# An attention and mixture-of-experts block: the softmax denominators given out by heads, and the shared expert's order in the second part changed

## The chip, the cores and the metric

The kernel is one program on one core of a Trainium2 chip. The metric is the device time of one execution in microseconds. The engines are PE (matmuls), DVE, ACT and POOL (elementwise and scalar work) and SP, whose queue issues most DMAs; they run side by side and wait for each other through semaphores.

## What is computed

The input is x, 4 batches of 512 rows of 512, and a context of 1601 rows a batch: 257 image rows and 1344 text rows. The block adds cross attention and then a mixture of experts.

```
q = rms_norm(LN(x) Wq + bq);  k, v from text rows;  k_img, v_img from image rows
attn = softmax(q k'/sqrt(32)) v  +  softmax(q k_img'/sqrt(32)) v_img      (16 heads of 32)
x = x + attn Wo + bo
h = LN(x)
router: sigmoid(h Wr), 8 groups, the best 3 of them, the best 4 of 32 experts, weights normed
each expert takes its first 80 tokens:  out[token] += w * (silu(h Wg) * (h Wu)) Wd
x = x + out + shared expert: (silu(h Sg) * (h Su)) Sd
```

The image and the text softmax have a denominator each, for every head and query.

## The kernel before

**Attention.** One batch after another goes through a projection stage and an attention stage. In the attention stage keys stand on partitions in 13 tiles of 128 (n = 0 to 12, in ORDER): n=0 is an image tile, n=1 the last 65 image rows, n=2 is mixed (its first 64 rows are text, the others image), and n=3 to 12 are text. The 16 heads are taken in 4 groups of 4. A step s is one tile of one group, and there are 52 steps a batch. In each step
- `scores(s + 2)` issues 12 f16 matmuls on PE: three products for each of 4 heads. A head has a row strip of the array (32 rows, all 128 columns), and the results go to two of three pairs of banks;
- ACT makes the exponentials of a step in two instructions (line 566), into one of four buffers `prob`;
- `weighted(s)` waits for the exponentials of step s (`a_exp`) and issues the numerators (line 1046): for each head an f32 matmul of the tile's values (up to 128 rows, 32 columns) with 512 queries. A head has a column strip of the array (all rows, 32 columns) and 32 partitions of bank NUM;
- the denominators (line 1053) are matmuls of the same form into bank DEN, with ones as weights. For image tiles and the mixed tile they read `prob` in steps n=0, 1 and 2, four heads each. For text tiles DVE first adds up the exponentials of n=3 to 12 in `sums`; the product with ones comes in the next group, at n=6 for the first 256 queries and at n=8 for the others, four heads each. For a batch's last group it stands behind the last step.

In the mixed step n=2 the numerators of the image half (rows 64 to 127) are issued, then the denominators over all 128 rows. DVE copies the image numerators out of NUM (line 764, `a_ni`). In n=3 the numerators of the mixed tile's text half follow, ahead of the tile's own. ACT waits for `a_av` before it overwrites a buffer of four steps ago; for the mixed tile it waits for the count of the step behind it, because that step reads the buffer last. The instructions on PE are in program order, written out by hand.

**The second part** (`ffn_program`) begins at about 967 us. It finishes the attention's output for the last batch (`output`, `out_rows`), norms its four row blocks and turns them for use as matmul operands:

- `out_norm(j)` on DVE writes `xn[j % 2]`, `norm_high` on ACT and `norm_low` on DVE split it into two f16 halves in `xs[j % 2]`, `turn_out(j)` on PE turns them, and SP stores xn to `table` in DRAM. With two buffers, out_norm(2) waits for the store of block 0 (`s_tab`).
- SP's queue holds, in this order: the input rows, the router's weights, a turned block, the three residual loads `x1s` (1 MB each), three of four parts of the weight ring (1.5 MB each), a wait, the fourth, and then the four stores.
- `gate_up(n)` on PE, n = 0 to 15, is 24 matmuls for quarter n % 4 of block n // 4; ACT makes a tanh (`gate_tanh`), DVE multiplies (`gate`, two instructions), ACT makes the high half and DVE the low half of `hs` (`gate_high`, `gate_low`).
- `down(bk)` on PE waits for all four quarters of its block (`f_lo`) and makes four products of 12 matmuls; DVE adds each to the residual (`residual`), and SP stores the result.
- Between these, DVE works out the router's choice in a long row of small instructions. From it come the slots: `one_hot(j)` on DVE makes a table for 128 tokens in one of two buffers, and `slots_of(j)` on PE multiplies it in (5 matmuls). ACT copies the sums out (`arow`), a DMA turns them, DVE makes indices (`e_idx`), and POOL gathers the experts' rows.
- POOL writes `ioS` by iota (2560 elements a partition) once the attention's low halves are there (`t_lo`).

Behind it a loop over 32 experts gathers rows, multiplies them and adds them to the result by indirect DMAs.

## Time and profile before

| | us |
|---|---|
| median of 3 runs (lowest, highest) | 1386.26 (1382.42, 1392.75) |
| the profiled execution | 1390.19 |
| its span, first to last instruction | 1388.3 |
| mean granted TensorE clock | 0.964 |
| PE busy | 1237.4 (89%) |
| DVE busy | 889.4 (64%) |
| ACT busy | 667.9 (48%) |
| POOL busy | 184.3 (13%) |

Matmuls are pipelined, so that PE's busy time is not PE at its peak. Line numbers (L1046) are those of the kernel printed above. An f32 matmul stands in the trace as two records, so four of them are "x8". The durations of single records overlap; the time from one start to the next says more. A number in square brackets is the idle time before a row, with who ended it.

### The profile page before, as it was taken

What the parts mean: (1) busy time and instruction counts of PE and PEld (TensorE: products, weight loads), DVE (VectorE), ACT (ScalarE), POOL (GpSimd) and SP (SyncE); (2) the same over time, 40 slices, a digit from 0 to 9 for tenths busy, and PEclk for the clock granted to TensorE, in tenths of its full rate; (3) what the DMA queues carried; (4) which work ended last, traced back from release to release, by engine and by line L of the source; (5) the groups of instructions that cost most, each with busy time, mean ns of one, the idle gap of its engine ahead of it and who ended that gap; (6) DMA issues with size and microseconds to landing.
All of it is one profiled execution on the core that took longest, in us unless ns stands there. A gap on an engine that the chain in (4) does not pass through costs nothing. (4 is left out here: it accounts for less than half of the span.)

```text
span 1388.3 us, 22059 instructions
## 1 busy us (share of the span) xinstructions
PE 1237.4 (89%) x8916; PEld 460.8 (33%) x8916; DVE 889.4 (64%) x1169; ACT 667.9 (48%) x910; POOL 184.3 (13%) x299
## 2 busy tenths in 40 slices
PE   4988999999999899989989998995778998988986
PEld 2542222444222245422224442221433333333332
DVE  5765877777587878757688776886666653222221
ACT  4546886345788534578853448883211011111111
POOL 0210000132000013200001320000210001333332
PEclk9999999999999999999999999997979999999999
DMA  7200000221000112200011122010800102899884
GB/s 276 84 25 15 2 2 7 85 69 69 24 1 1 51 41 69 92 1 1 2 64 36 61 76 92 1 62 25 337 8 31 39 0 82 279 289 311 288 283 110
DMA packets 38388, 117.80 MB, mean 85 GB/s; under 512 B 6544, under 2 KB 6800, under 8 KB 33040
## 3 DMA queue, kind: packets, MB, share of 16 engines
q1 hardware_dynamic: 33168, 105.60, 21.5%
q0 software_dynamic: 5120, 10.82, 3.7%
q8 instruction: 68, 1.11, 0.3%
q14 instruction: 32, 0.26, 0.1%
HBM read 95.67 MB, written 20.73 MB: 84 GB/s over the span
## 5 line engine op out<-in xcount | busy, mean ns | idle before, releaser
L566 ACT ACTIVATE work<-ps 128x1024 f32<-128x1024 f32 (+1 forms) x416 | 403.1, 1021 | 61.0 <-PE ps L1039 58.7
L1046 PE MATMUL ps<-work,vals 128*32 128x512 f32 (+2 forms) x1792 | 236.6, 604 | 0.9 <-ACT work L566 0.8
L862 PE MATMUL ps<-wts,work 128*128 128x512 f16 x864 | 205.3, 389 | 14.6 <-DVE work L595 14.6
L1039 PE MATMUL ps<-quer,keys 32*128 32x512 f16 x2496 | 171.8, 377 | 25.1 <-ACT work L566 9.3
L778 DVE TENSOR_TENSOR work<-work 128x2048 f32<-128x2048 f32 x64 | 146.6, 2291 | 11.4 <-ACT work L566 7.3
L778 DVE TENSOR_TENSOR attn<-attn,work 128x2048 f32<-128x2048 f32 x64 | 146.6, 2290 | 10.8 <-ACT work L566 7.3
L862 PE MATMUL ps<-wts,hl 128*128 128x512 f16 x480 | 116.1, 395 | 23.2 <-DVE hl L595 23.2
L862 PEld LDWEIGHTS ps<-wts,work 128*128 128x128 f16 x864 | 83.7, 100 | 116.6 <-issue 16.9
L1039 PEld LDWEIGHTS ps<-quer,keys 32*128 32x128 f16 x2496 | 46.2, 92 | 214.5 <-ACT work L566 189.2
L1786 PE MATMUL f_ps<-wring,xgt 128*80 128x512 f32 x256 | 117.1, 601 | 0.0
L1372 ACT ACTIVATE yf<-f_ps,wc 80x512 f32<-80x512 f32 x32 | 21.9, 683 | 171.3 <-PE f_ps L1801 143.3
L418 POOL TENSOR_SCALAR small<-small 128x1 f32<-128x1 f32 x68 | 13.7, 201 | 651.1 <-ACT work L486 651.1
L486 ACT ACTIVATE work<-work 128x512 f32<-128x512 f32 x68 | 42.8, 630 | 116.4 <-DVE work L612 116.4
L481 ACT CAST work<-work 128x512 f16<-128x512 f32 x68 | 42.0, 617 | 105.8 <-DVE work L625 105.4
L625 DVE SCALAR_TENSOR_TENSOR work<-work,small,vec 128x512 f32<-128x512 f32 (+1 forms) x72 | 63.6, 883 | 43.7 <-POOL small L421 43.6
L631 DVE TENSOR_TENSOR work<-work 128x512 f16<-128x512 f32 x68 | 47.0, 692 | 44.5 <-ACT work L481 44.4
L862 PEld LDWEIGHTS ps<-wts,hl 128*128 128x128 f16 x480 | 47.0, 101 | 84.0 <-issue 38.3
L1046 PEld LDWEIGHTS ps<-work,vals 128*32 128x32 f32 (+2 forms) x1792 | 35.9, 107 | 105.6 <-issue 89.9
L1629 DVE SCALAR_TENSOR_TENSOR hh<-eg,f_ps 80x256 f32<-80x256 f32 x32 | 13.3, 417 | 85.4 <-ACT eg L1367 85.4
L1801 PE MATMUL f_ps<-wring,ht 128*80 128x512 f32 x128 | 63.0, 615 | 3.5 <-DVE ht L1633 0.8
L1294 POOL DMA_INDIRECT out<-yf,idx x32 | 45.6, 1426 | 145.0 <-DMA out<-yf,idx 93.1
L1786 PEld LDWEIGHTS f_ps<-wring,xgt 128*80 128x80 f32 x256 | 39.1, 153 | 73.5 <-issue 73.5
(208 smaller groups left out, 1445.7 us busy)
## 6 DMA issues: line engine op xcount, KB each, us to landing
wring<-in_wx SPq DMA_DIRECT2D x32, 1536.0 KB, 7.9
raw<-in_ctx SPq DMA_DIRECT2D x52, 256.0 KB, 2.8
work<-in_x SPq DMA_DIRECT2D x4, 1024.0 KB, 5.5
table<-nums SPq DMA_DIRECT2D x16, 256.0 KB, 2.3
out<-x1s SPq DMA_DIRECT2D x16, 256.0 KB, 2.3
work<-in_x SPq DMA_DIRECT2D x12, 256.0 KB, 4.9
x<-work SPq DMA_DIRECT2D x12, 256.0 KB, 2.0
x2t_rows<-nums SPq DMA_DIRECT2D x12, 256.0 KB, 2.5
```

The source lines that it names most:

```text
L481: act.copy(stack[i % 2][:, 0, :], kraw[i % 2]).then_inc(k_hi, 1)
L486: act.activation(junk, kraw[i % 2], ACT.Square, accum_out=ssq[i % 2]).then_inc(k_sq, 1)
L566: act.activation(prob[0:rows, s % PROBS, 2 * half:2 * half + 2, :], ps[0:rows, 2 * pair:2 * pair + 2, :], ACT.Exp, scale=SCALE).then_inc(a ...
L625: ins = dve.scalar_tensor_tensor(kraw[i % 2][a:z, :], kraw[i % 2][a:z, :], rin[i % 2][a:z, :], vec[a:z, weight, :], ALU.mult, ALU.mult)
L631: dve.tensor_tensor(stack[i % 2][:, 1, :], kraw[i % 2], stack[i % 2][:, 0, :], ALU.subtract).then_inc(k_lo, 1)
L778: dve.tensor_tensor(acc, acc, cur, ALU.add).then_inc(a_sum, 1)
L862: mm = pe.matmul(out, lhs(a, c)[:, cols], wts[:, w, z, c * D:(c + 1) * D], start=(k == 0), stop=(k == len(steps) - 1))
L1039: mm = pe.matmul(ps[:, 2 * pair + h % 2, :], k[h * HD:(h + 1) * HD, :], q[h * HD:(h + 1) * HD, :], start=(e == 0), stop=(e == len(terms) - 1))
L1046: mm = pe.matmul(ps[h * HD:(h + 1) * HD, NUM, :], vals[a:z, ORDER[n], g * P + h * HD:g * P + (h + 1) * HD], prob[a:z, s % PROBS, h, :], st ...
L1294: pool.indirect_dma_start(out=out[:, :], out_offset=bass.IndirectOffsetOnAxis(ap=idx[:, n - 1:n], axis=0), in_=yf[(n - 1) % 2][:, :], in_o ...
L1786: mm = pe.matmul(ps[0:CAP, 7 if u % 2 == 0 else 0, :], xgt[u % 2][:, c, :], wring[:, u, c * 512:(c + 1) * 512], start=(c == 0), stop=(c == ...
L1801: mm = pe.matmul(ps[0:CAP, 2 + u % 2, :], ht[u % 2][:, c, :], wring[:, u, 2048 + c * D:2048 + (c + 1) * D], start=(c == 0), stop=(c == 1))
```

## The change

In the attention stage:
- The image denominators of n=0 are issued for heads 0 to 2 in their own step and for head 3 at the start of n=1, behind the next scores and ahead of the wait for the exponentials. Those of n=1 are issued for heads 0 and 1 in their step and for 2 and 3 at the start of n=2. The signal `a_av` moves with them.
- In the mixed tile each numerator of one half of the rows is paired with the denominator of the other half: in n=2 the image numerators (rows 64 to 127) with the denominator over rows 0 to 63, for four heads in turn; the text numerators (rows 0 to 63) with the denominator over rows 64 to 127, heads 0 and 1 at the end of n=3, behind the tile's own numerators, and heads 2 and 3 at the start of n=4.
- The text denominators of the group before are issued for one head over all 512 queries in each of n=6, 7, 8 and 9.

In the second part:
- xn and xs have four buffers; out_norm and norm_high lose their waits, and one semaphore counts all four stores. The three residual loads move behind the stores in SP's queue, and every `residual` waits for all three.
- POOL's iota waits for the last turn (`n_turn`).
- gate_up(4) moves ahead of the down products of block 0, gate_up(8) ahead of those of block 1; DVE and ACT follow.
- A down product is split: `down_first` issues three of four chunks of the first two products ahead of the wait for the last low half, `down_last` the other two products.
- The slot search goes two row blocks at a time behind each gate_up, and slots 12 to 15 stand behind gate_up(13) and gate_up(14); DVE makes one_hot(12) to (15) behind gate(13) and gate(14) and their low halves, and the indices behind gate_low(15).
- PE no longer waits for all residuals before the experts.

```diff
...
-                def denominator(g, kind, src, rows, a=0, z=L, first=False, last=False):
-                    for h in range(4):
-                        mm = pe.matmul(ps[h * HD:(h + 1) * HD, DEN, a:z], ones[0:rows, kind, g, :],
-                                       src[0:rows, h, a:z], start=first, stop=last)
-                    return mm
+                def image_part(s, h, rows, first=False):
+                    return pe.matmul(ps[h * HD:(h + 1) * HD, DEN, :], ones[0:rows, 1, s // KT, :],
+                                     prob[0:rows, s % PROBS, h, :], start=first, stop=False)
+
+                def mixed_part(s, h, a, z):
+                    return pe.matmul(ps[h * HD:(h + 1) * HD, DEN, :], ones[a:z, 2, s // KT, :],
+                                     prob[a:z, s % PROBS, h, :], start=False, stop=False)
+
+                def text_part(g, h, last=False):
+                    return pe.matmul(ps[h * HD:(h + 1) * HD, DEN, :], ones[:, 0, g, :], sums[g % 2][:, h, :],
+                                     start=False, stop=last)
+
+                def mixed_text(s, h):
+                    numerator(s, h, 0, SPLIT, False, False)
+                    return mixed_part(s, h, SPLIT, P)
 
                 def weighted(s):
                     g, n = s // KT, s % KT
+                    if n == 1:
+                        image_part(s - 1, 3, P, first=(g == 0)).then_inc(a_av, 1)
+                    if n == 2:
+                        image_part(s - 1, 2, LAST)
+                        image_part(s - 1, 3, LAST).then_inc(a_av, 1)
+                    if n == 4:
+                        mixed_text(s - 2, 2).then_inc(a_av, 1)
+                        mixed_text(s - 2, 3).then_inc(a_av, 1)
                     pe.wait_ge(a_exp, unit(bb, 2 * s + 1))
                     if n == 0:
                         if g == 0:
@@ -1064,26 +1085,30 @@
                                 pe.wait_ge(n_out, xn(out_batch(bb - 1), QT - 1))
                         else:
                             pe.wait_ge(a_nt, gn(bb, g - 1))
-                        numerator(s, 0, P, True, False)
-                        denominator(g, 1, prob[:, s % PROBS, :, :], P, first=(g == 0)).then_inc(a_av, 1)
+                        numerators(s, P, True, False)
+                        for h in range(3):
+                            image_part(s, h, P, first=(g == 0))
                     elif n == 1:
-                        numerator(s, 0, LAST, False, False)
-                        denominator(g, 1, prob[:, s % PROBS, :, :], LAST).then_inc(a_av, 1)
+                        numerators(s, LAST, False, False)
+                        image_part(s, 0, LAST)
+                        image_part(s, 1, LAST)
                     elif n == 2:
-                        numerator(s, SPLIT, P, False, True).then_inc(a_img, 1)
-                        denominator(g, 2, prob[:, s % PROBS, :, :], P).then_inc(a_av, 1)
+                        for h in range(4):
+                            mm = numerator(s, h, SPLIT, P, False, True)
+                            mixed_part(s, h, 0, SPLIT)
+                        mm.then_inc(a_img, 1)
                     elif n == 3:
                         pe.wait_ge(a_ni, gn(bb, g))
-                        numerator(s - 1, 0, SPLIT, True, False)
-                        numerator(s, 0, P, False, False).then_inc(a_av, 1)
+                        numerators(s, P, True, False)
+                        mixed_text(s - 1, 0)
+                        mixed_text(s - 1, 1)
                     else:
-                        numerator(s, 0, P, False, n == KT - 1).then_inc(a_av, 1)
-                        if g > 0 and n in (6, 8):
+                        numerators(s, P, False, n == KT - 1).then_inc(a_av, 1)
+                        if g > 0 and 6 <= n < 10:
                             if n == 6:
                                 pe.wait_ge(a_sum, added(bb, g - 1, ADDS - 1))
-                            at = 0 if n == 6 else L // 2
-                            mm = denominator(g - 1, 0, sums[(g - 1) % 2], P, at, at + L // 2)
-                            if n == 8:
+                            mm = text_part(g - 1, n - 6)
+                            if n == 9:
                                 mm.then_inc(a_den, 1)
...
-        xn = [spare[:, j, :] for j in range(2)]
-        xs = [spare[:, 2 + j, :].bitcast(F16).rearrange("p (s n) -> p s n", s=2) for j in range(2)]
+        xn = [spare[:, j, :] for j in range(QT)]
+        xs = [spare[:, QT + j, :].bitcast(F16).rearrange("p (s n) -> p s n", s=2) for j in range(QT)]
...
-            for k in range(B - 1):
-                sp.dma_start(x1s[k][:, :, :], x1_dram[k * L:(k + 1) * L, :].rearrange("(j p) n -> p j n", p=P)).then_inc(
-                    s_xl, 16)
...
-                sp.dma_start(table[(LB + j) * P:(LB + j + 1) * P, 0:D], xn[j % 2]).then_inc(s_tab[j % 2], 16)
+                sp.dma_start(table[(LB + j) * P:(LB + j + 1) * P, 0:D], xn[j]).then_inc(s_tab, 16)
+            for k in range(B - 1):
+                sp.dma_start(x1s[k][:, :, :], x1_dram[k * L:(k + 1) * L, :].rearrange("(j p) n -> p j n", p=P)).then_inc(
+                    s_xl, 16)
...
-            pool.wait_ge(t_lo, NG)
+            pool.wait_ge(n_turn, QT)
...
             def norm_high(j):
                 act.wait_ge(n_norm, j + 1)
-                upto(act, n_turn, j - 1)
-                act.copy(xs[j % 2][:, 0, :], xn[j % 2]).then_inc(n_hi, 1)
+                act.copy(xs[j][:, 0, :], xn[j]).then_inc(n_hi, 1)
...
-                dve.wait_ge(s_xl, 16 * min(bk + 1, B - 1))
+                dve.wait_ge(s_xl, 16 * (B - 1))
...
             residual(1)
+            gate_low(8)
...
-            for j in range(2):
-                dve.wait_ge(s_tab[j], 32)
+            dve.wait_ge(s_tab, 16 * QT)
             one_hot(0)
             one_hot(1)
             chain(TT(fl(wv), fl(wv), fl(tmp), ALU.mult))
             dve.sem_inc(e_wv, 1)
-            gate(8)
-            gate_low(8)
-            for j in (2, 3, 4):
-                one_hot(j)
-            gate(9)
-            gate_low(9)
-            for j in (5, 6, 7):
-                one_hot(j)
-            gate(10)
-            gate_low(10)
-            for j in (8, 9, 10):
-                one_hot(j)
-            gate(11)
-            gate_low(11)
-            for j in (11, 12):
-                one_hot(j)
+            for n in range(9, 13):
+                gate(n)
+                if n < 12:
+                    gate_low(n)
+                one_hot(2 * (n - 8))
+                one_hot(2 * (n - 8) + 1)
             residual(2)
-            for j in (13, 14, 15):
-                one_hot(j)
-            gate(12)
             gate_low(12)
+            one_hot(10)
+            one_hot(11)
             gate(13)
             gate_low(13)
+            for j in (12, 13):
+                one_hot(j)
+            gate(14)
+            gate_low(14)
+            for j in (14, 15):
+                one_hot(j)
+            gate(15)
+            gate_low(15)
             dve.wait_ge(s_ia, 16)
             chain(dve.tensor_scalar(ib[:, :], ia[:, :], 0.0, None, ALU.is_equal))
             chain(dve.tensor_scalar(ib[:, :], ib[:, :], sio[0:CAP, 0:1], None, ALU.mult))
             chain(dve.scalar_tensor_tensor(ib[:, :], ia[:, :], float(T), ib[:, :], ALU.add, ALU.add))
             dve.tensor_copy(idx[:, :], ib[:, :]).then_inc(e_idx, 1)
-            gate(14)
-            gate_low(14)
-            gate(15)
-            gate_low(15)
             residual(3)
...
-            def down(bk):
+            def down_part(bk, q, chunks):
+                for c in chunks:
+                    for a, z in PARTS:
+                        mm = pe.matmul(ps[:, 4 + q % 2, :], hs[:, a, c, q * P:(q + 1) * P],
+                                       swt[SD][:, z, c * D:(c + 1) * D], start=(c == 0 and (a, z) == PARTS[0]),
+                                       stop=(c == NI - 1 and (a, z) == PARTS[-1]))
+                return mm
+
+            def down_first(bk):
+                pe.wait_ge(f_lo, bk * NI + NI - 1)
+                if bk == 0:
+                    pe.wait_ge(n_out, QT)
+                for q in range(2):
+                    upto(pe, f_ac, bk * 4 + q - 1)
+                    down_part(bk, q, range(NI - 1))
                 pe.wait_ge(f_lo, bk * NI + NI)
-                for q in range(4):
-                    n = bk * 4 + q + 1
-                    upto(pe, f_ac, n - 2)
-                    if n <= 2:
-                        pe.wait_ge(n_out, QT)
-                    product(ps[:, 4 + q % 2, :], lambda a, c: hs[:, a, c, q * P:(q + 1) * P],
-                            lambda z, c: swt[SD][:, z, c * D:(c + 1) * D], NI).then_inc(f_dn, 1)
+                for q in range(2):
+                    down_part(bk, q, (NI - 1,)).then_inc(f_dn, 1)
+
+            def down_last(bk):
+                for q in range(2, 4):
+                    pe.wait_ge(f_ac, bk * 4 + q - 1)
+                    down_part(bk, q, range(NI)).then_inc(f_dn, 1)
 
...
-            for n in range(1, 4):
+            for n in range(1, 5):
                 gate_up(n)
-            down(0)
-            for n in range(4, 8):
+            down_first(0)
+            down_last(0)
+            for n in range(5, 9):
                 gate_up(n)
-            down(1)
+            down_first(1)
+            down_last(1)
             pe.wait_ge(s_const, N_CONST)
             pe.wait_ge(e_m16, 1)
             flat = lambda t: t[:, :, :].rearrange("p j e -> p (j e)")
             pe.wait_ge(e_ez, 1)
             pe.matmul(ps[:, POSITION, :], before[:, :], flat(m16), start=True, stop=False)
             pe.matmul(ps[:, POSITION, :], ones16[:, :], flat(c16), start=False, stop=True).then_inc(e_pos, 1)
-            gate_up(8)
-            slots_of(0)
-            slots_of(1)
-            gate_up(9)
-            for j in (2, 3, 4):
-                slots_of(j)
-            gate_up(10)
-            for j in (5, 6, 7):
-                slots_of(j)
-            gate_up(11)
-            for j in (8, 9, 10):
-                slots_of(j)
-            gate_up(12)
-            down(2)
-            for j in (11, 12):
-                slots_of(j)
+            for n in range(9, 13):
+                gate_up(n)
+                slots_of(2 * (n - 9))
+                slots_of(2 * (n - 9) + 1)
+            down_first(2)
+            slots_of(8)
+            slots_of(9)
+            down_last(2)
+            slots_of(10)
+            slots_of(11)
             gate_up(13)
-            for j in (13, 14, 15):
-                slots_of(j)
+            slots_of(12)
+            slots_of(13)
             gate_up(14)
+            slots_of(14)
+            slots_of(15)
             gate_up(15)
-            down(3)
+            down_first(3)
+            down_last(3)
...
-            pe.wait_ge(f_ac, NT)
```

## Rows read from the trace of the kernel before

**Rows 1.** Windows of the stages, first attention and second part (busy us, granted clock).
```profile
...
117.00:230.50 113.50, 107.33 (x1187) 24.27 (x1188) 81.10 (x43) 98.33 (x103) 0.00 (x0) 1.00 0.01 2
...
967.00:1171.00 204.00, 171.35 (x950) 76.48 (x950) 122.07 (x272) 31.42 (x50) 16.96 (x27) 0.91 0.24 87
...
```

**Rows 2.** Timeline of PE, steps n=0 to n=4 of a group (start, us, what).
```profile
...
208.21 1.07 PE L1046 MATMUL ps<-work,vals 128*32 128x512 f32 x8
209.07 1.07 PE L1053 MATMUL ps<-work,ones 128*32 128x512 f32 x8
210.07 0.83 PE L1039 MATMUL ps<-quer,keys 32*128 32x512 f16 x12
...
212.68 0.83 PE L1039 MATMUL ps<-quer,keys 32*128 32x512 f16 x12
213.43 1.06 PE L1046 MATMUL ps<-work,vals 64*32 64x512 f32 x8
214.43 1.06 PE L1053 MATMUL ps<-work,ones 128*32 128x512 f32 x8
...
218.17 0.82 PE L1039 MATMUL ps<-quer,keys 32*128 32x512 f16 x12
...
220.13 0.83 PE L1039 MATMUL ps<-quer,keys 32*128 32x512 f16 x12
...
```

**Rows 3.** Timeline of ACT in the same stretch.
```profile
...
216.30 1.94 ACT L566 ACTIVATE work<-ps 128x1024 f32<-128x1024 f32 x2 [0.81 <-PE ps L1039]
...
```

**Rows 4.** Timeline of PE, steps n=6 and n=7 of the group before.
```profile
...
193.21 0.83 PE L1039 MATMUL ps<-quer,keys 32*128 32x512 f16 x12
...
195.40 0.83 PE L1039 MATMUL ps<-quer,keys 32*128 32x512 f16 x12
...
197.35 0.83 PE L1039 MATMUL ps<-quer,keys 32*128 32x512 f16 x12
...
```

**Rows 5.** Timeline of PE, full-array f32 matmuls at the second part's start.
```profile
...
974.02 1.02 PE L1661 MATMUL f_ps<-rcp,sel 128*128 128x512 f32 x2
974.88 1.02 PE L1662 MATMUL f_ps<-rcp,sel 128*128 128x512 f32 x2
...
```

**Rows 6.** Timeline of PE in the second part, with its stalls.
```profile
...
1005.91 1.01 PE L1681 MATMUL f_ps<-ident,nums 128*128 128x128 f16 x8 [5.70 <-DVE x1s L1413]
1011.96 1.04 PE L1681 MATMUL f_ps<-ident,nums 128*128 128x128 f16 x8 [5.04 <-DVE nums L1427]
...
1035.79 13.42 PE L1656 MATMUL f_ps<-sd,hs 128*128 128x512 f16 x48 [4.01 <-DVE hs L1441]
...
1075.17 12.52 PE L1656 MATMUL f_ps<-sd,hs 128*128 128x512 f16 x48 [5.24 <-DVE hs L1441]
...
1101.64 0.59 PE L1715 MATMUL f_ps<-oneh,tok 128*1 128x512 f16 x5 [1.15 <-DVE oneh L1573]
...
1123.33 10.52 PE L1656 MATMUL f_ps<-sd,hs 128*128 128x512 f16 x48
...
1159.25 10.53 PE L1656 MATMUL f_ps<-sd,hs 128*128 128x512 f16 x48 [3.51 <-DVE hs L1441]
...
```

**Rows 7.** Windows of the second part, granted clock behind a stall.
```profile
...
1036.00:1040.00 4.00, 4.00 (x10) 1.36 (x9) 3.60 (x35) 0.00 (x0) 0.00 (x0) 0.50 0.00 0
...
```

**Rows 8.** Timeline of DVE in the attention stretch of rows 2.
```profile
...
214.56 0.69 DVE L764 COPY nums<-ps 128x512 f32<-128x512 f32 x1 [4.30 <-PE ps L1046]
...
```

**Rows 9.** Chain of work that ended last, norms of the second part.
```profile
...
990.59 12.56 DMA table<-nums
...
1003.25 0.56 DVE nums L1423
...
1007.66 2.88 DVE nums L1423
...
```

**Rows 10.** Timeline of DVE, a one-hot of the slot search.
```profile
...
1140.66 1.49 DVE L1573 TENSOR_TENSOR oneh<-ioS,pv 128x2560 f16<-128x2560 f16 x1 [3.27 <-PE f_ps L1715]
...
```

**Rows 11.** DMA issues (count, median us from issue to landing): the gathers.
```profile
...
xg<-table,idx POOLq DMA_INDIRECT x32, 5.0
...
```

More of the change, by code:

```diff
@@ L1041, in scores, with numerator, numerators @@
                     mm.then_inc(a_sc, 1)
-                def numerator(s, a, z, first, last):
+                def numerator(s, h, a, z, first, last):
                     g, n = s // KT, s % KT
+                    return pe.matmul(ps[h * HD:(h + 1) * HD, NUM, :],
+                                     vals[a:z, ORDER[n], g * P + h * HD:g * P + (h + 1) * HD],
+                                     prob[a:z, s % PROBS, h, :], start=first, stop=last)
+                def numerators(s, rows, first, last):
@@ L1098, in attention @@
                 pe.wait_ge(a_sum, added(bb, NG - 1, ADDS - 1))
-                denominator(NG - 1, 0, sums[(NG - 1) % 2], P, last=True).then_inc(a_den, 1)
+                for h in range(4):
+                    mm = text_part(NG - 1, h, last=True)
+                mm.then_inc(a_den, 1)
             def one_pass(p):
@@ L1351, in _ @@
                            scale=-1.0 / WS).then_inc(e_ez, 1)
-            for n in range(1, 14):
+            for n in range(1, 15):
                 gate_tanh(n)
@@ L1359, in _ @@
             cp.then_inc(e_ar, 1)
-            for n in range(14, 4 * NI):
+            for n in range(15, 4 * NI):
                 gate_tanh(n)
@@ L1527, in _ @@
             chain(TT(gt[0][:, :, :], gt[0][:, :, :], gt[1][:, :, :], ALU.add))
+            gate(4)
             residual(0)
+            gate_low(4)
             chain(TT(masked[:, :, :].rearrange("p j (g k) -> p (j g) k", k=4), q4,
@@ L1551, in _ @@
                 if j == 5:
-                    gate(7)
-                if j == 10:
-                    gate_low(7)
+                    gate(8)
             dve.sem_inc(e_m16, 1)
```

29 lines of the change are left out of this document (12 added, 17 removed).

## The prediction, made before the changed kernel was built or run

> **What bounds the kernel now.** I read the windows of the stages first [rows 1]. Each of the four attention stages takes 113.5 us; PE is busy for 107.3 of them and ACT, which makes the exponentials, for 98.3. So the two stand close to each other and neither covers the other wholly. The second part's first 204 us (the shared expert, the router and the slot search) have PE busy for 171.
>
> The timeline of PE tells how a key step is made [rows 2]. From one group of score matmuls to the next it is 2.61 us (210.07 to 212.68) in the image step n=1, 2.75 each in the mixed steps n=2 and n=3 (5.49 together, to 218.17), but 1.96 in n=4 (218.17 to 220.13). The 1.96 is ACT's own pace: in the long steps it stands idle for 0.81 us before its pair of exponentials [rows 3]. In the steps that carry the text denominators it is 2.19, in the one after it 1.95 [rows 4]. So a step lasts as long as PE's work in it or 1.96, whichever is more; scores run at most two steps ahead in three pairs of banks, and no slack is carried from step to step.
>
> PE's work in a step is made of rounds. The four matmuls of a round (one a head, four column strips of the array) start together, and the next four follow 0.86 us later (208.21 to 209.07) [rows 2]. One f32 matmul over the full array, alone, also takes 0.86 (974.02 to 974.88) [rows 5]. **A round costs the time of one matmul, whether it fills four strips or one.** Where the tile's shape changes it takes about 0.14 more: 1.00 from the 64-row round to the 128-row one (213.43 to 214.43).
>
> In the second part the timeline of PE has its stalls [rows 6]: 5.70 and 5.04 before the turns of the last norms, 4.01 and 5.24 before the down products of blocks 0 and 1, 3.51 before block 3's, and 1.15 before a slot search (four such). The first two down products then take 13.42 and 12.52 instead of 10.52, since the clock had fallen: it is 0.50 (the 1.2 GHz level) at 1036 to 1040 [rows 7]. A stall of some 3 us or more costs 1.7 to 2.9 behind itself.
>
> **Attention, step by step.** Between two score groups the array must be clear, since scores use all columns of their row strip and a denominator all rows of its column strip. I count for each step the longest strip, in rounds.
> - n=0: before, four numerators and four denominators, 2 rounds. After, four and three: strips 0 to 2 still hold two. No change.
> - n=1: the fourth denominator of step 0 now stands ahead, then four numerators and two denominators: again 2 rounds at best. No change.
> - n=2: two left denominators (128-row shape), then the 64-row pairs, all heads side by side if tiles of both row halves run at once: 2 rounds and two changes of shape, as before (2.75).
> - n=3: four numerators, then the pairs of heads 0 and 1: 2 rounds, 2.75 as before.
> - n=4: the pairs of heads 2 and 3, then four numerators: 2 rounds where there was 1. The step goes from 1.96 to 2.75, **+0.79**.
> - n=6 to 9, for all but a batch's first group: before, n=6 and n=8 carried four matmuls of 256 columns, half a round (2.19), n=7 and n=9 nothing (1.96). After, each carries one head's 512 columns, a full round for one strip: 0.75 for the scores, 2 rounds, 0.14 for the shape, which is the 2.61 of n=1. **+0.42, +0.65, +0.42, +0.65 = +2.14.**
>
> The pairing thus removes work (8 strip-rounds a strip where there were 9 in n=0 to 4), but the work is laid out so that each score group closes another half-empty round. Two waits are added to this. The exponentials two steps past n=4 need the buffers of n=2 and n=3, which now come free only behind the pairs in n=4, a round after that step's scores rather than before them. By the 0.81 that ACT already idles [rows 3] I put this at 0.2 of delay; it is between 0 and 0.4. And DVE copies the image numerators, 0.69 us [rows 8], after n=2's last round; PE's next numerators come a score group and a gap later, about as late. I take 0, and 0.2 as the most. DVE's additions get more time.
>
> Sum: 12 groups x (0.79 + 2.14 + 0.2) = 37.6, and 4 first groups x (0.79 + 0.2) = 4.0. **Attention +41.6 us**, between 38 (no delays) and 47. A batch's last denominators stay four heads in one round.
>
> By the Trainium skill (TensorEngine Tiling (Array Packing), Key Properties) changing the tiling mode drains TensorE while tiles of one mode run independently. The first agrees with the 1.00 against 0.86 above. The second, with the eight tiles of 64x32 that it lists, is what lets the pairs share a round; no row here shows eight at once, and without it n=2 to 4 would each take a round more.
>
> **The second part.** Removed:
> - Norms: out_norm(2) stood behind the store of the first row block, 12.56 us from issue to landing among 3 MB of residual and 6 MB of expert loads [rows 9]. With four buffers it goes when its scale is ready, 3.1 earlier, and the last norm no longer takes 2.88 beside POOL's iota, against 0.56: the last turn comes some **5.35** earlier. The iota runs while DVE waits for the router's exponentials. The residual loads now leave SP's queue after the four stores, near 1005, need some 10 us and are first used near 1035; the loads of the weight ring ahead of them keep their place. Cost 0 by that cover; up to 5 if they slipped past it.
> - Down products: block 0's stall and slow clock, 4.0 + 2.9, go, since another gate-up (24 matmuls, 5.2 us) stands ahead of it. Block 1's 5.2 + 2.0 likewise. Block 3's 3.5 is covered by the first three chunks of two products (3.9). Block 2 had none.
> - Slot search: two a round instead of three take away four stalls of 1.15, and a short stall with a slow stretch behind it at 1143, which I take as 2.4 by the ones above. Together **30.0** us.
>
> Added: DVE must now make one-hots behind gates that wait for the same gate-up. (a) Slots 10 and 11 wait for the last residual of block 2, its low half and two one-hots of 1.49 [rows 10]: 4.4. (b) Slots 12 and 13 come directly behind gate-up 13 on PE, while DVE does gate(13) and its low half first. That chain is the 3.51 seen before block 3's down [rows 6], plus a one-hot 1.49, plus the second's excess over a slot matmul group, 0.9: 5.9. (c) The same for slots 14 and 15: 5.9. (d) Three such stalls would lower the clock again: 5, between 0 and 8. Together **21.2**. So the second part gains 8.8; with the bounds of the clock and of (a), 5 to 16.
>
> The experts' gathers then become the next to be late: DVE makes the index after gate_low(15); ACT and a DMA have the slot table ready by then, and a gather needs 5.0 us from issue to landing [rows 11]. I get a landing within 0 to 2 us of the end of the last down product. I take 0, since the wait for all residuals ahead of the experts (0.79) is gone. The expert loop itself is untouched.
>
> **Sum.** +41.6 - 8.8 = +32.8; against the profiled execution's 1390.19 us (span 1388.3) that gives 1423. That run lies 3.9 above the median of the three; on the median of 1386.26 I round to **1418**.
>
> **Rivals.**
> 1. *A lone column strip leaves room for the scores* (the faster side). If score matmuls could start in strips that are free, a denominator of one head would cost nothing beyond ACT's pace. With every step at 1.96, a group falls by 3.4 (four steps near 2.7 and two of 2.19 go to 1.96, or 28.9 to 25.5) and a first group by 2.9: -52, and with the second part 1325; half of it, 1350 to 1370. It decides from the point where attention gives back the 9 us, 0.6 a group. For it speaks that PE had been given such fillers ahead of waits; against it that a row strip's scores cross every column, and that nothing in the trace overlaps two shapes. Chance 0.08.
> 2. *The pairs don't run side by side.* Then n=2, 3 and 4 take a round more each: 16 x 3 x 0.86 = +41, so 1459. The scores show four row strips at once and the numerators four column strips, never both. Chance 0.08.
> 3. *The new stalls at the slots are mild.* If DVE gets ahead and no clock falls, the second part gains 20 to 30 and attention costs only 38: 1394 to 1404. Against it stands the order on DVE, one queue. Chance 0.10.
> 4. *The fillers fit in waits*, so that attention doesn't change and only the second part shows: 1377. Against: there are no waits of PE in n=0 to 3. Chance 0.04.
>
> My forecast, 1405 to 1440, has 0.70. With the upper end of rival 3 the range is 1396 to 1440, with some 0.8. No measurement of this kernel tells less than about 1% apart (13.9 us; the three runs span 10). Faster by over 1%: rival 1 and a part of 4, 0.09. Within 1%, up to 1400: half of rival 3 and the rest of 4, 0.08. Slower: 0.83.
>
> **What would show it.** In the profile after: steps of 2.61 in n=6 to 9 and 2.75 in n=4, a group of 32.0 us instead of 28.9 (the sum of its 13 steps), and ACT idle for 0.6 to 0.8 before its pair in n=4 and n=6 to 9, where it now goes through. A group below 29 makes rival 1 or 4 right, one near 34.5 rival 2. In the second part: no wait for the table store, no stall before blocks 0, 1 and 3, and instead stalls of PE of 4 to 6 us at slots 10, 12 and 14. What would make the prediction wrong most easily is the assumption that a round with one strip costs as much as one with four, since each is seen in the trace, but never the lone strip itself.

## The result and the profile after

The kernel after the change took **1425.4 us** (median of 4 runs, 1424.54 to 1426.79), the kernel before, on the same chip, 1387.72 (4 runs, 1382.42 to 1392.75). The ratio is 1.027, with a 95% interval of 1.0238 to 1.0302: slower by 2.7%. The forecast was 1418, between 1396 and 1440. The profiled execution after took 1424.54 us, span 1422.8, mean granted clock 0.974 (before: 1388.3 and 0.964).

First the windows, as in [rows 1]: the first attention stage, the projection stage between the third and the fourth attention stage, and the second part. A row gives the length, the busy time of PE, PEld, DVE, ACT and POOL with the count of instructions, the granted clock, the DMA share and GB/s.

```profile
118.75:243.50 124.75, 118.90 (x1196) 26.06 (x1200) 83.07 (x44) 98.88 (x103) 0.00 (x0) 1.00 0.01 1
...
741.58:864.65 123.07, 114.07 (x693) 55.12 (x693) 93.32 (x139) 51.59 (x99) 26.14 (x54) 0.99 0.21 67
...
1008.75:1207.06 198.31, 171.65 (x947) 75.23 (x948) 118.70 (x271) 31.62 (x50) 16.81 (x27) 0.92 0.24 88
```

The attention stage is 11.3 us longer than the one in [rows 1]. ACT works as long as before (98.9 against 98.3), and PE is busy for 11.6 more. In the profile page's list of the costliest groups ACT's idle time ahead of its exponentials is now 109.3 us (it was 61.0), 73.2 of it put down to the scores on PE.

```profile
L566 ACT ACTIVATE work<-ps 128x1024 f32<-128x1024 f32 (+1 forms) x416 | 403.1, 1021 | 109.3 <-PE ps L1039 73.2
```

The steps show where, in the timeline of PE for the last batch, from the scores ahead of n=2 to those behind n=9 (start, us, what, [idle before, who ended it]). It answers to [rows 2, 4].

```profile
968.28 0.83 PE L1039 MATMUL ps<-quer,keys 32*128 32x512 f16 x12
...
970.02 0.61 PE L1045 MATMUL ps<-work,vals 64*32 64x512 f32 x1
...
970.07 0.61 PE L1059 MATMUL ps<-work,ones 64*32 64x512 f32 x1
...
971.04 0.83 PE L1039 MATMUL ps<-quer,keys 32*128 32x512 f16 x12
972.04 1.61 PE L1045 MATMUL ps<-work,vals 128*32 128x512 f32 x9 [0.17 <-DVE nums L764]
...
974.03 0.83 PE L1039 MATMUL ps<-quer,keys 32*128 32x512 f16 x12
...
977.08 0.83 PE L1039 MATMUL ps<-quer,keys 32*128 32x512 f16 x12 [0.24 <-ACT work L566]
...
979.04 0.83 PE L1039 MATMUL ps<-quer,keys 32*128 32x512 f16 x12
979.79 1.07 PE L1045 MATMUL ps<-work,vals 128*32 128x512 f32 x8
980.68 1.02 PE L1063 MATMUL ps<-work,ones 128*32 128x512 f32 x2
981.63 0.83 PE L1039 MATMUL ps<-quer,keys 32*128 32x512 f16 x12
```

Read from one start of scores (L1039) to the next: n=2 takes 2.76, n=3 2.99 (a wait of 0.17 for DVE's copy is in it), n=4 3.05 (with 0.24 for ACT), n=5 1.96 and n=6 2.59, in which one head's denominator, "x2", follows the numerators by a round (0.89). The next three steps take 2.60, 2.61 and 2.61. A group is 32.34 us, where it was 28.90; a batch's first group 29.69, where it was 28.35. ACT's own timeline shows what stands behind the 0.24: ahead of its next pair it stood idle for 2.14 us, the first part of it for the scores of n=4 (they end at 974.86), the last 1.1 till the pairs in n=4 (L1059) had read their buffer.

```profile
976.00 5.85 ACT L566 ACTIVATE work<-ps 128x1024 f32<-128x1024 f32 x6 [2.14 <-PE ps L1059]
```

Then the second part, which answers to [rows 6].

```profile
1047.69 1.03 PE L1698 MATMUL f_ps<-ident,nums 128*128 128x128 f16 x8 [3.12 <-DVE nums L1451]
...
1112.69 7.04 PE L1719 MATMUL f_ps<-sd,hs 128*128 128x512 f16 x24 [3.89 <-DVE x1s L1473]
...
1159.83 0.59 PE L1746 MATMUL f_ps<-oneh,tok 128*1 128x512 f16 x5 [2.89 <-DVE oneh L1598]
1161.22 0.62 PE L1746 MATMUL f_ps<-oneh,tok 128*1 128x512 f16 x5 [0.81 <-DVE oneh L1598]
1161.78 4.37 PE L1673 MATMUL f_ps<-x2t,sg 128*128 128x512 f16 x12
...
1173.65 1.01 PE L1746 MATMUL f_ps<-oneh,tok 128*1 128x512 f16 x5 [4.91 <-DVE oneh L1598]
1175.05 1.01 PE L1746 MATMUL f_ps<-oneh,tok 128*1 128x512 f16 x5 [0.39 <-DVE oneh L1598]
1176.00 4.09 PE L1673 MATMUL f_ps<-x2t,sg 128*128 128x512 f16 x12
...
1187.59 1.01 PE L1746 MATMUL f_ps<-oneh,tok 128*1 128x512 f16 x5 [4.91 <-DVE oneh L1598]
...
1189.93 3.95 PE L1673 MATMUL f_ps<-x2t,sg 128*128 128x512 f16 x12
```

The waits ahead of the last norms' turns, of the down products and of the early slots are gone or smaller. In their place stand 3.7, 5.3 and 5.3 us at the slots 10, 12 and 14, each with a slow product behind it (4.37, 4.09 and 3.95 instead of 2.75), and one that was not foreseen: 3.89 in the middle of block 1's down products, whose second half then takes 7.04 instead of 5.35.

**The account of the span** (starts read from both timelines): the four attention stages +48.2 (452.3 to 500.5, each up to the start of its last group of scores), the three projection stages between them −6.1 (377.5 to 371.4), the end of attention −1.2, the second part up to the first expert −4.6, the experts −2.0, the beginning +0.2. Together +34.5, which is 1422.8 less 1388.3.

### The profile page after: what moved, and what is told of

It is laid out like the page before. It is cut to its first block and busy times, and to the rows that moved or that the text cites. A ratio compares the mean times of both kernels' runs of the same rounds, so it can differ in the third digit from the quotient of the medians.

```text
span 1422.8 us, 22117 instructions
## 1 busy us (share of the span) xinstructions
PE 1275.7 (90%) x8948; PEld 464.2 (33%) x8948; DVE 885.0 (62%) x1169; ACT 668.3 (47%) x910; POOL 184.0 (13%) x299
## 3 DMA queue, kind: packets, MB, share of 16 engines
q1 hardware_dynamic: 33168, 105.60, 21.2%
## 5 line engine op out<-in xcount | busy, mean ns | idle before, releaser
L566 ACT ACTIVATE work<-ps 128x1024 f32<-128x1024 f32 (+1 forms) x416 | 403.1, 1021 | 109.3 <-PE ps L1039 73.2
L1045 PE MATMUL ps<-work,vals 128*32 128x512 f32 (+2 forms) x1792 | 266.8, 605 | 3.7 <-DVE nums L764 2.7
L1039 PE MATMUL ps<-quer,keys 32*128 32x512 f16 x2496 | 172.5, 379 | 23.2 <-ACT work L566 13.0
L1039 PEld LDWEIGHTS ps<-quer,keys 32*128 32x128 f16 x2496 | 46.3, 92 | 221.4 <-ACT work L566 196.1
L486 ACT ACTIVATE work<-work 128x512 f32<-128x512 f32 x68 | 42.8, 630 | 116.6 <-DVE work L612 116.6
L1045 PEld LDWEIGHTS ps<-work,vals 128*32 128x32 f32 (+2 forms) x1792 | 42.4, 107 | 132.4 <-issue 127.2
L764 DVE COPY nums<-ps 128x512 f32<-128x512 f32 x16 | 11.1, 692 | 97.8 <-PE ps L1045 97.8
L1055 PE MATMUL ps<-work,ones 128*32 128x512 f32 (+1 forms) x256 | 64.4, 597 | 0.0
```

Of the source, the lines that this page charges most:

```text
L486: act.activation(junk, kraw[i % 2], ACT.Square, accum_out=ssq[i % 2]).then_inc(k_sq, 1)
L566: act.activation(prob[0:rows, s % PROBS, 2 * half:2 * half + 2, :], ps[0:rows, 2 * pair:2 * pair + 2, :], ACT.Exp, scale=SCALE).then_inc(a ...
L1039: mm = pe.matmul(ps[:, 2 * pair + h % 2, :], k[h * HD:(h + 1) * HD, :], q[h * HD:(h + 1) * HD, :], start=(e == 0), stop=(e == len(terms) - 1))
L1045: return pe.matmul(ps[h * HD:(h + 1) * HD, NUM, :], vals[a:z, ORDER[n], g * P + h * HD:g * P + (h + 1) * HD], prob[a:z, s % PROBS, h, :], ...
L1055: return pe.matmul(ps[h * HD:(h + 1) * HD, DEN, :], ones[0:rows, 1, s // KT, :], prob[0:rows, s % PROBS, h, :], start=first, stop=False)
```

## Experiments

The times are medians, the ratios against the kernel before in runs on the same chip. "Attention" is the sum of the four stages, each from its first to its last score matmul, and "second" runs from the second part's first matmul to the first expert, both from the one profiled execution. "Slow" is the time at the lower clock level, worked out as twice the span times (1 − mean granted clock).

| kernel | us | ratio (95%) | attention | second | slow |
|---|---|---|---|---|---|
| before | 1387.44 to 1389.35, by chip | 1 | 454.1 | 202.9 | 100 |
| after | 1425.4 | 1.027 (1.0238 to 1.0302) | 502.3 | 198.3 | 74 |
| e_attn | 1431.69 | 1.0302 (1.0268 to 1.0337) | 502.3 | 200.3 | 77 |
| e_second | 1383.93 | 0.9972 (0.9951 to 0.9992) | 454.1 | 197.8 | 94 |
| e_text2 | 1412.3 | 1.016 (1.0127 to 1.0193) | 485.5 | 197.9 | 90 |
| e_text4 | 1406.37 | 1.0117 (1.0077 to 1.0157) | 479.2 | 199.4 | 87 |
| e_pairs3 | 1414.45 | 1.0186 (1.0156 to 1.0216) | 484.1 | 199.2 | 84 |
| e_image | 1412.28 | 1.0177 (1.015 to 1.0205) | 491.7 | 197.6 | 87 |
| e_whole | 1373.73 | 0.9898 (0.9857 to 0.9939) | 443.2 | 203.2 | 88 |
| e_quart | 1374.9 | 0.9918 (0.9891 to 0.9946) | 438.4 | 205.7 | 104 |
| e_slots | 1365.8 | 0.9836 (0.9807 to 0.9864) | 454.2 | 180.0 | 79 |
| e_res | 1379.32 | 0.9927 (0.9905 to 0.9948) | 455.7 | 194.5 | 99 |
| e_best | 1347.62 | 0.9714 (0.9696 to 0.9733) | 438.4 | 176.0 | 56 |

The profiled executions of e_pairs3 (1406.75) and e_best (1336.38) were the fastest of their runs, 8 and 11 us below the medians; their stages are those of these executions.

**The two halves of the change.** e_attn is the attention of after with the second part of before, e_second the reverse.

> The new attention with the second part of the kernel before. Theory of rounds: the steps are those of the changed kernel (2.60 in n=6 to 9, 3.05 in n=4, 32.3 us a group), and the whole lies 41 to 48 us above the kernel before, 1429 to 1436. Rival, the two parts disturb each other: clearly less or more than the changed kernel's time plus the second part's own gain.

> The attention of the kernel before with the new second part alone. By the changed kernel's trace the second part (first instruction to the first turn of an expert's rows) goes from 202.9 to about 198.3, so 1380 to 1384. The prediction's own figure was a gain of 8.8 (5 to 16). Rival: the moved residual loads or the iota cost something that the attention's state hid, no gain.

Attention alone costs 42.8 us and the second part alone gives back 5.0. Together that is +37.8, and the whole change measured +37.7: within the some 4 us that the intervals leave open, the halves don't act on each other. The attention alone is all of the loss.

**Text denominators, two heads or four a step.** From the kernel after:

```diff
-                        if g > 0 and 6 <= n < 10:
+                        if g > 0 and n in (6, 8):
...
-                            mm = text_part(g - 1, n - 6)
-                            if n == 9:
+                            for h in range(n - 6, n - 4):
+                                mm = text_part(g - 1, h)
+                            if n == 8:
...
```

In e_text4 the condition is `n == 6`, and all four heads are issued there.

> The changed kernel, with the four text denominators issued as heads 0 and 1 in n=6 and heads 2 and 3 in n=8; the same matmuls, only grouped. Theory of rounds: n=6 and n=8 stay at 2.60, n=7 and n=9 go to 1.96; 1.28 less in each of 12 groups, 15.4 in all, about 1410. Rival, each matmul has a price of its own (its issue, its weight load) or the new waits take the time: no change in the sum, 1425.

> The changed kernel, with all four heads' text denominators in n=6. Theory of rounds: n=6 stays at 2.60 with four matmuls where it was 2.60 with one, n=7 to 9 go to 1.96; 1.93 less in each of 12 groups, 23.1 in all, about 1402. Rival, a price for each matmul: n=6 grows to about 4.5 and the sum stays near 1425.

The timeline of PE of e_text2, step n=6, and then that of e_text4:

```profile
197.92 0.83 PE L1039 MATMUL ps<-quer,keys 32*128 32x512 f16 x12
...
199.56 1.03 PE L1063 MATMUL ps<-attn,ones 128*32 128x512 f32 x4
200.52 0.83 PE L1039 MATMUL ps<-quer,keys 32*128 32x512 f16 x12
```

```profile
197.69 0.83 PE L1039 MATMUL ps<-quer,keys 32*128 32x512 f16 x12
...
199.33 1.04 PE L1063 MATMUL ps<-attn,ones 128*32 128x512 f32 x8
200.30 0.83 PE L1039 MATMUL ps<-quer,keys 32*128 32x512 f16 x12
```

One head's denominator (x2), two (x4) and four (x8) all make a step of 2.59 to 2.61. This is the lone strip that the trace of before never showed, and it settles the first rival: the scores don't start in the strips that are free. The time goes with the number of steps that carry a round: four in after, two, one. By the steps, 12 groups save 1.28 each in e_text2 and 1.92 in e_text4, 15.4 and 23.0; the stages fell by 16.8 (in after one stage had a slow n=0 of 1.4, shown below; e_text2 had none) and 23.1. The medians fell by less, 13.1 and 19.0, and lie 2 and 4 us above what was expected.

**The mixed tile's text pairs all in n=3.** In the kernel after, the block ahead of n=4's wait goes, and n=3 issues `mixed_text` for four heads. In n=2 the pair's denominator goes ahead of its numerator, so that `a_img` covers both.

```diff
-                    if n == 4:
-                        mixed_text(s - 2, 2).then_inc(a_av, 1)
-                        mixed_text(s - 2, 3).then_inc(a_av, 1)
...
-                        mixed_text(s - 1, 0)
-                        mixed_text(s - 1, 1)
+                        for h in range(4):
+                            mm = mixed_text(s - 1, h)
...
```

> The changed kernel, with the mixed tile's text pairs of heads 2 and 3 moved from the start of n=4 to the end of n=3, so that all four heads share a round there; within a pair of n=2 the denominator comes ahead of the numerator. Theory of rounds: n=4 goes from 3.05 to 1.96, of which 0.3 is ACT's wait for the buffers of n=2 and n=3 that n=4's pairs released late; n=3 stays at 2.99. 1.09 in each of 16 groups, 17.4 in all, about 1408. Rival, eight tiles at once can't keep up with more than four pairs' rows: n=3 grows by up to 0.9 and little is gained.

Its timeline of PE, n=3 and n=4:

```profile
219.87 0.83 PE L1039 MATMUL ps<-quer,keys 32*128 32x512 f16 x12
220.88 1.61 PE L1045 MATMUL ps<-work,vals 128*32 128x512 f32 x9 [0.19 <-DVE nums L764]
...
222.90 0.83 PE L1039 MATMUL ps<-quer,keys 32*128 32x512 f16 x12
...
224.86 0.83 PE L1039 MATMUL ps<-quer,keys 32*128 32x512 f16 x12
```

n=3 with twice the pairs takes 3.03 (2.99 with half of them), and n=4 is back at 1.96. So n=4's round and its wait for buffers were worth 1.09 a group, 17.4 us over 16 groups; the stages fell by 18.2. The median fell by less, 10.9, to 6 us above what was expected; its runs lay between 1406.75 and 1416.08, and the profile of the fastest can't say what the others lost.

**The image denominators whole, in their own steps.** From after: the blocks for n=1 and n=2 ahead of the wait go, n=0 and n=1 issue `image_part` for four heads.

> The changed kernel, with the image denominators of n=0 and n=1 issued for all four heads in their own steps. Theory of rounds: n=0 and n=1 stay at 2.69 and 2.61, two rounds with seven matmuls or with eight; n=2 loses the round of two left denominators and falls from 2.76 to 1.96; n=3 stays near 2.99 or loses 0.1. 0.8 in each of 16 groups, 13 in all, about 1412. Rival, a price for each matmul: n=0 and n=1 grow by what n=2 loses, 1425.

Its timeline of PE from the scores ahead of n=0 to those behind n=2:

```profile
183.02 0.83 PE L1039 MATMUL ps<-quer,keys 32*128 32x512 f16 x12
...
184.72 1.07 PE L1055 MATMUL ps<-work,ones 128*32 128x512 f32 x8
185.72 0.83 PE L1039 MATMUL ps<-quer,keys 32*128 32x512 f16 x12
...
188.33 0.83 PE L1039 MATMUL ps<-quer,keys 32*128 32x512 f16 x12
...
190.29 0.83 PE L1039 MATMUL ps<-quer,keys 32*128 32x512 f16 x12
```

n=0 takes 2.70 with four denominators and 2.69 with three, n=1 2.61 both times: the heads that the change had moved out of these steps saved nothing there, and in n=2 they filled a round of their own (2.76 against 1.96 without them). A group falls by 0.97: 0.80 in n=2 and 0.18 in n=3, which is 2.81 here instead of 2.99. Over 16 groups that is 15.5, but the stages fell by only 10.6, since n=0 of every batch's first group took 4.1 to 4.3 here instead of 2.6. A window of that place, 860 to 863, has the clock granted at 0.65. In after the same happened in one stage of four, and so it did in e_text4 (4.0) and in e_res (4.3), which has the attention of before. The window of after:

```profile
619.00:623.40 4.40, 4.04 (x30) 0.83 (x34) 0.00 (x0) 3.16 (x4) 0.00 (x0) 0.62 0.01 4
```

**Every round whole.** e_whole has the edits of e_pairs3 and e_image, the text denominators as before the change (four heads, 256 columns each, in n=6 and n=8) and the second part of before. Only the pairs of the mixed tile are left of the change. e_quart spreads the text denominators over n=6 to 9 in 128 columns each; its edit against e_whole:

```diff
-                        if g > 0 and n in (6, 8):
+                        if g > 0 and n in (6, 7, 8, 9):
...
-                            at = (6, 8).index(n) * 256
+                            at = (6, 7, 8, 9).index(n) * 128
...
```

> Attention in whole rounds: image denominators of n=0 and n=1 with four heads in their own steps, the mixed tile paired with all four heads in n=2 and in n=3, text denominators in halves of the queries in n=6 and n=8 as before; the second part is that of the kernel before. Theory of rounds: against the kernel before n=2 falls from 2.75 to ACT's 1.96 and nothing else grows but n=3 by up to 0.2 (DVE's copy of the image numerators is due sooner); 0.6 to 0.8 in each of 16 groups, so 1375 to 1378. Rival, pairing itself has a cost (eight tiles at once): no gain, 1388 or more.

> As the kernel with whole rounds, but the text denominators given out by quarters of the queries (128 columns, four heads each) in n=6 to 9. Theory of rounds: PE's work in such a step is 0.75 + 0.86 + 0.21 + 0.14 = 1.97, which is ACT's pace, so n=6 and n=8 fall from 2.19 to 1.97 and n=7 and n=9 stay within 0.03; 0.4 in each of 12 groups, 5 in all, about 1369. Rival: a matmul of 128 columns has a fixed cost that makes it as long as one of 256, and four such steps of 2.19 make it 6 slower than the kernel with whole rounds.

The timeline of PE of e_whole, step n=2, then that of e_quart, step n=6:

```profile
210.50 0.83 PE L1039 MATMUL ps<-quer,keys 32*128 32x512 f16 x12
211.26 0.61 PE L1059 MATMUL ps<-work,ones 64*32 64x512 f32 x1
...
211.30 0.61 PE L1045 MATMUL ps<-work,vals 64*32 64x512 f32 x1
...
212.46 0.83 PE L1039 MATMUL ps<-quer,keys 32*128 32x512 f16 x12
```

```profile
217.81 0.83 PE L1039 MATMUL ps<-quer,keys 32*128 32x512 f16 x12
...
219.45 0.40 PE L1063 MATMUL ps<-work,ones 128*32 128x128 f32 x8
219.78 0.83 PE L1039 MATMUL ps<-quer,keys 32*128 32x512 f16 x12
```

In e_whole the mixed tile's pairing does what it is for. Eight tiles of 64x32 start within 0.04 us and n=2 runs at ACT's pace. The attention stages are 10.9 shorter than before, and the kernel is faster than before by 1.0%. (Its span is 14.7 shorter; 2.7 of the rest lies in the projection stages, whose instructions are those of before.) In e_quart the steps n=6 to 9 are 1.97 each. So with four heads a step is 1.97, 2.19 or 2.61 for 128, 256 or 512 columns. The differences, 0.22 and 0.42, are a quarter and a half of the 0.86 of a round, so the time goes with the columns. That also speaks against a rival that was not tested by itself, a fixed price for each step that carries denominators. The stages fall by another 4.8, but the whole time, expected at 1369, didn't: the two medians are 1.2 us apart and their intervals overlap. Its time at the lower clock was 104 us against 88; the projection stages were 3.9 us longer, the end of attention 1.5 and the second part 2.5, the experts 5.8 shorter. That the clock took the gain is argued from these sums, not shown.

**The slots a gate-up later.** From e_second: `gate_up(13)` stands ahead of slots 10 and 11, `gate_up(14)` ahead of 12 and 13, `gate_up(15)` ahead of 14 and 15; ACT makes the tanh of n=15 before it copies the slots out.

```diff
+                gate_up(13)
                 slots_of(10)
                 slots_of(11)
-                gate_up(13)
+                gate_up(14)
                 slots_of(12)
                 slots_of(13)
-                gate_up(14)
+                gate_up(15)
...
-                gate_up(15)
```

> Attention of the kernel before and the new second part, with the slot search of PE one gate-up later: slots 10 and 11 behind gate_up(13), 12 and 13 behind gate_up(14), 14 and 15 behind gate_up(15), and ACT's copies of the slot table behind the last high half. Theory: the stalls at slots 10, 12 and 14 (3.7 + 5.3 + 5.3) and the slow clock behind them go, some 18; the gathers come later against the last down product and give 2 to 5 back. 12 to 16 below the second part's own kernel, about 1369. Rival: the gathers, not the stalls, set when the experts start: the same time as that kernel.

```profile
1119.57 1.02 PE L1716 MATMUL f_ps<-oneh,tok 128*1 128x512 f16 x10
...
1125.81 1.02 PE L1716 MATMUL f_ps<-oneh,tok 128*1 128x512 f16 x10
...
1132.05 1.02 PE L1716 MATMUL f_ps<-oneh,tok 128*1 128x512 f16 x10
...
1141.33 5.35 PE L1689 MATMUL f_ps<-sd,hs 128*128 128x512 f16 x24 [2.97 <-DVE x1s L1443]
```

In its timeline of PE the three slot pairs go through without a wait. The second part takes 180.0 instead of 197.8, and the median falls by 18.1, a little more than expected. From the second half of block 2's down product to the first of block 3's, the stretch that holds the three slot pairs, PE takes 23.9 us where e_second took 44.5 and after 44.7. So the order had cost 20.6 in e_second: 3.7 + 5.3 + 5.3 of waits, 3.6 in the slow products behind them, and the rest in the slot matmuls themselves, five of which took up to 1.01 instead of 0.59 (in after the clock was granted at 0.50 from 1173.65 to 1176.00).

Of the 20.6, 2.8 came back, though not at the gathers: PE now waits 2.97 in block 3's down product (0.21 in e_second) for a residual that stands on DVE behind the slot indices. DVE's timeline shows it waiting for the DMA that turns the slot table:

```profile
1139.79 0.18 DVE L1597 TENSOR_SCALAR ib<-ia 80x32 f32<-80x32 f32 x1 [4.22 <-DMA ia<-arow]
```

e_best has the same wait of 2.98.

**Half of block 1's residual earlier on DVE.** From e_second: `residual(1)` is split. Its first two quarters go directly behind `dve.sem_inc(e_m16, 1)`, ahead of the router's next stretch of small instructions, the others stay where they were.

> Attention of the kernel before and the new second part, with the first two residual additions of block 1 ahead of five router instructions on DVE instead of behind them. The changed kernel's trace shows PE waiting 3.9 us in the middle of down product 1 for the first of these additions, then 1.7 lost to a lower clock. Theory, DVE arrives late: the wait falls to about 1.2 and the clock holds, 4 less than the second part's own kernel. Rival, the wait is for something else or is made up for later by the one-hots: no difference.

The timelines of PE at block 1's second half, e_second and then e_res:

```profile
1069.79 7.04 PE L1692 MATMUL f_ps<-sd,hs 128*128 128x512 f16 x24 [3.88 <-DVE x1s L1446]
```

```profile
1070.22 5.35 PE L1693 MATMUL f_ps<-sd,hs 128*128 128x512 f16 x24 [1.28 <-DVE x1s L1446]
```

The wait falls by 2.60 and the product by 1.69; the median fell by 4.6. (In the profiled executions the second part fell by 3.3, since the products behind the slot stalls were slower there, 4.54, 4.18 and 4.00 against 4.06, 3.94 and 3.87.) So the unforeseen stall is DVE's order: the bank that `down_last` writes is free only when DVE has added its old content, and DVE was in the router's row.

**All of it together.** e_best has the attention of e_quart and the second part of e_slots and e_res.

> All of it: whole rounds in attention with text denominators by quarters, the new second part with the slot search one gate-up later and the first residual additions of block 1 ahead of the router's instructions. If the parts add up: attention stage 454 to about 438, second part 203 to about 177, 1388 to about 1346 (1342 to 1352). Rival: the gathers or the one-hots eat what the earlier residual gives, so no more than the sum of the two separate ones, 1352 to 1358.

It took 1347.62 us, as the parts added up had it (1342 to 1352), 2.9% less than the kernel before and 77.8 less than the kernel after.

## Why the prediction held, and where it was off

- **A round costs the time of one matmul, whether it fills four strips or one**: right, and the step on which the sum hung. e_text2 and e_text4 show it directly, e_pairs3 and e_image for the other rounds. The four steps rose by 2.11 a group, where 2.14 was put. Rival 1 falls.
- **n=0 to n=2 unchanged**: right (2.69, 2.61 and 2.76).
- **The pairs side by side**: right; rival 2 falls. What the prediction takes from the Trainium skill (TensorEngine Tiling (Array Packing), Key Properties), that tiles operate independently, agrees with eight starts between 970.02 and 970.07.
- **n=4, +0.79 and 0.2 for the buffers**: the round was right, the wait was put too low. The step went from 1.96 to 3.05, so the wait is 0.30. e_pairs3 takes both away.
- **DVE's copy of the image numerators, 0**: wrong. PE waits 0.17 for it, and n=3 is 2.99 instead of 2.75, 0.24 a group. The two waits together are 0.34 more than put, 5.4 us over 16 groups; with one slow n=0 of 1.4 (the clock at 0.62) they turn the forecast 41.6 into the 48.2 measured. The upper bound was put at 47; by its own terms (38.3 and 0.6 in each of 16 groups) it is 47.9, and the measured value lies just above that too.
- **The second part, −8.8**: it gave 4.6. The norms were right: from the second part's start to its last turn 38.94 instead of 44.31, 5.37 less where 5.35 was put. The stalls at the slots came where they were expected and nearly at their size: the waits are 14.3 and the slow products 4.2, and with the slot matmuls, which ran slow too, the stretch is 20.8 longer than in e_slots, where 21.2 was put. What failed is that no wait was put behind block 1: 3.9 and 1.7, shown by e_res. I had followed who waits for DVE's low half, not who waits for its `residual` behind the router. Of what came out better than put, 0.5 is the product behind the last turn (3.85, where it was 4.38), 0.8 the wait ahead of the experts that is gone, and 0.4 the slots; 0.3 us is left over. Rival 3 falls: the stalls were there, and e_slots shows what they cost.
- **"A stall of some 3 us or more costs 1.7 to 2.9 behind itself"**: a wrong reading of its own rows. In [rows 6] the stall of 3.51 ahead of block 3 is followed by 10.53, the full speed. In the runs 2.97 (e_slots) was followed by 5.35, and 3.88 (e_second) by 7.04. That the 5 put for the clock behind the three new stalls came out near the measured 4.2 (5.9 with the slow slot matmuls) is thus partly luck: all three happened to be followed by a slow stretch.
- **The projection stages, not considered**: they gave 6.1 back, and the end of attention 1.2. In both kernels a product follows a wait of 1.99 for the same operand, about 11 us ahead of the fourth attention stage; it stands first in the timeline of before and then in that of after:

```profile
822.73 4.44 PE L862 MATMUL ps<-wts,hl 128*128 128x512 f16 x12 [1.99 <-DVE hl L595]
```

```profile
855.04 2.75 PE L862 MATMUL ps<-wts,hl 128*128 128x512 f16 x12 [1.99 <-DVE hl L595]
```

Behind it the clock is granted at 0.57 (822.73 to 826.20), so mostly at the lower level (1.2 GHz), in one, and at 1.00, the full 2.4 GHz, in the other, 1.7 us apart. That stage is 2.7 us shorter (123.07 at 0.99, where it was 125.78 at 0.96). PE stands idle in it for 9.1 and 9.0 us; its busy time fell from 116.7 to 114.1 with the same instructions. Over the whole span the lower level held for 74 us instead of 100. So this gain comes from the clock; why it was granted differently isn't settled by any run here.
- **Rival 4** (no change in attention, 1377) falls with e_attn.

The sum of the forecast was +32.8; the span rose by 34.5 and the medians by 37.7. (On the median of 1386.26 that sum gives 1419, not 1418.) That the sum came so close is in part luck. Attention cost 6.6 more than put and the second part gave 4.2 less, both outside their own ranges; the projection stages, the end of attention and the experts, for which nothing was put, gave back 6.1, 1.2 and 2.0. Without them the span would have risen by some 44. The direction and the mechanism, rounds in attention, don't rest on that.

## What to carry to other kernels

Count packed matmuls in rounds, and count rounds for each stretch between two groups of another shape: work taken out of a full round saves nothing, and work put into a step without a free place in a round costs a whole one, even if it is one tile of four. To spread work over steps, cut its columns, not its tiles. And when an engine's order is changed, ask for each instruction of the slower engine who waits for it, the freeing of banks included; PE should have one piece of independent work between a producer's input and the matmul that needs its output. An instruction that others wait for should not stand behind one that waits itself: in e_slots and e_best block 3's residual does.

## What was not expected of the hardware

- A wait of PE has no fixed price behind it. The same wait of 1.99 us was followed by a product of 4.44 us or of 2.75, and 1.28 (e_res) and 2.97 (e_slots) by one of 5.35, where 3.88 (e_second) was followed by 7.04.
- A stretch of low clock can repeat at one place of a loop: with whole image rounds (e_image) the first n=0 of every batch took 4.1 to 4.3 us instead of 2.6, four times in one execution (the clock was 0.65 in the window read); e_whole, with the same image rounds and the pairs moved too, had 2.61 there. Each is one profiled execution, and the same place was slow once in after, e_text4 and e_res. So that the edit brought it there is not shown.
